# A diagonal state-space layer and an LSTM block: the order of work behind the last products

## The reference, cut to what matters

```python
x = L0_attn_r                                   # (8, 2048, 512) float32
x = x + _layernorm(_L0_attn_ref(_layernorm(x)))  # state-space convolution over the sequence, gelu
x = x + _layernorm(_L0_ffn_ref(_layernorm(x)))   # the block below
...
def step(c, xt):                                 # the scan runs over axis 0, of length 8
    ft = sigmoid(xt @ wf.T + c @ uf.T + bf)
    it = sigmoid(xt @ wi.T + c @ ui.T + bi)
    gt = tanh(xt @ wc.T + c @ uc.T + bc)
    return ft * c + it * gt, None
c_final, _ = lax.scan(step, c0, x)
h = tanh(einsum('tbi,oi->tbo', x, wo) + c_final @ uo.T + bo)
```

## Time and profile before

| | us |
|---|---|
| median of 3 executions | 2649.8 |
| lowest and highest of them | 2649.52 and 2650.55 |
| the profiled execution's own time | 2650.23 |
| its span, from the first to the last instruction | 2648.6 |
| TensorE busy (share of span) | 2526.6 (95%) |
| VectorE | 1841.0 (70%) |
| ScalarE | 1623.0 (61%) |
| GpSimd | 1133.2 (43%) |
| granted TensorE clock, mean, as a part of the full one | 0.982 |

### The profile page before, as it was taken

How to read it: one execution, slowest core, us unless ns; L and a number is a source line. 1 busy time by engine, 2 the same in 40 slices (tenths; PEclk the granted TensorE clock), 3 DMA queues, 4 the chain that set the end, 5 groups by cost and what they waited for, 6 DMA issues and landing times.

```text
span 2648.6 us, 57574 instructions
## 1 busy us (share of the span) xinstructions
PE 2526.6 (95%) x22659; PEld 2205.2 (83%) x22659; DVE 1841.0 (70%) x3413; ACT 1623.0 (61%) x3003; POOL 1133.2 (43%) x1437
## 2 busy tenths in 40 slices
PE   5499999997899999999999999999999999999997
PEld 4278888886788888888888888888888888888886
DVE  7855556558887677766777887776677764467666
ACT  8656667567665555555556665555555553378777
POOL 7768686725332223222234332322223220068667
PEclk9799999998999999999999999999999999999999
DMA  8779797889674556445655755544555432489998
GB/s 355 286 227 312 267 314 270 271 293 343 181 196 116 130 139 167 119 116 131 141 167 150 204 152 143 166 116 116 135 137 168 119 82 49 168 333 362 370 359 321
DMA packets 507551, 542.52 MB, mean 205 GB/s; under 512 B 273936, under 2 KB 412944, under 8 KB 488720
## 3 DMA queue, kind: packets, MB, share of 16 engines
q1 hardware_dynamic: 507280, 538.85, 65.3%
HBM read 292.88 MB, written 180.88 MB: 179 GB/s over the span
## 4 chain that ended last, share of the span: by engine, by line
PE 84%; DVE 4%; POOL 4%; ACT 3%; DMA 3%; issue 2%; SPq 1%; DVEq 0%; POOLq 0%; ACTq 0%
PE bank L2138 31%; PE bank L2148 29%; PE bank L2194 8%; PE bank L2027 4%; PE bank L1977 3%; PE bank L2013 3%; PE bank L2035 2%; PE bank L1989 2%; PE bank L2169 2%; DVE big L1827 1%; PE bank L1997 1%; ACT big L1343 1%; POOL big L886 1%; POOL big L990 1%; DVE big L1884 1%
## 5 line engine op out<-in xcount | busy, mean ns | idle before, releaser
L2138 PE MATMUL bank<-big 128*128 128x256 f16 x8064 | 1078.8, 273 | 20.8 <-ACT big L1387 8.3
L2148 PE MATMUL bank<-big 128*128 128x256 f16 x7056 | 962.5, 273 | 0.0
L2138 PEld LDWEIGHTS bank<-big 128*128 128x128 f16 x8064 | 790.4, 98 | 117.4 <-ACT big L1387 9.9
L2148 PEld LDWEIGHTS bank<-big 128*128 128x128 f16 x7056 | 690.4, 98 | 79.9
L1031 POOL TENSOR_SCALAR big<-big 128x1 f32<-128x1 f32 x253 | 108.0, 427 | 1084.8 <-DVE big L1674 806.4
L1884 DVE TENSOR_TENSOR big<-bank,big 128x512 f32<-128x512 f32 x256 | 175.1, 684 | 197.1 <-PE bank L2148 195.0
L2194 PE MATMUL bank<-big 128*128 128x256 f16 x2688 | 295.3, 273 | 4.4 <-ACT bank L1323 4.0
L1299 ACT ACTIVATE big<-big 128x512 f32<-128x512 f32 x384 | 289.6, 803 | 13.5 <-DVE big L1884 13.4
L2194 PEld LDWEIGHTS bank<-big 128*128 128x128 f16 x2688 | 262.4, 98 | 37.0 <-ACT bank L1323 4.9
L1870 DVE TENSOR_TENSOR big<-bank,big 128x512 f32<-128x512 f32 x256 | 176.3, 689 | 140.9 <-PE bank L2148 118.5
L1231 ACT ACTIVATE big<-big 128x512 f32<-128x512 f32 x256 | 205.9, 808 | 100.3 <-POOL big L1033 96.5
(11 more groups left out here) (233 smaller groups left out, 3724.3 us busy)
## 6 DMA issues: line engine op xcount, KB each, us to landing
xtd<-big SPq DMA_DIRECT2D x60, 1024.0 KB, 7.0
big<-xr SPq DMA_DIRECT2D x16, 2048.0 KB, 8.7
big<-xg SPq DMA_DIRECT2D x64, 512.0 KB, 7.8
big<-kpad SPq DMA_DIRECT2D x32, 1024.0 KB, 12.2
yd<-big SPq DMA_DIRECT2D x16, 2048.0 KB, 16.8
big<-x SPq DMA_DIRECT2D x128, 256.0 KB, 3.1
x1d<-big SPq DMA_DIRECT2D x128, 256.0 KB, 3.1
big<-x1d SPq DMA_DIRECT2D x64, 512.0 KB, 8.5
```

Of the source, the lines that this page charges most:

```text
L2138: ins = e.matmul(o, WX[2 * g + lw][:, q, kt, 128 * a:128 * a + 128], slot[u % 2][:, part, lx, k0 + kt, :], start=(first and kt == 0 and (l ...
L2148: ins = e.matmul(o, WC[2 * g + lw][:, q, kt, 128 * a:128 * a + 128], cc[unit(u)[1] % 2][:, qc, lx, kt, :], start=False, stop=end, skip_gro ...
```

## The change

Three edits behind the last products, and what they need in other places:

1. On VectorE, in turn m = 64, both closing sums of pair 63 come ahead of both statistics of pair 62.
2. On ScalarE, in turn m = 64, the tanh of pair 63 (both halves) comes ahead of the normalization of pair 61.
3. The residual sums of pairs 61 and 62 go from GpSimd to VectorE, behind all statistics and ahead of the sums of pair 63. SP waits for `hfin` for them. GpSimd makes the rates of pair 63 in one pass for both halves.

```diff
+POOL_PAIRS = PAIRS - 3
...
                 if m < PAIRS - 1:
-                    w.wait_ge(s["hres"], m + 1)
+                    if m < POOL_PAIRS:
+                        w.wait_ge(s["hres"], m + 1)
+                    else:
+                        w.wait_ge(s["hfin"], m - POOL_PAIRS + 1)
                     e.dma_start(o, rb[m % NRB]).then_inc(s[f"rb{m % NRB}"], 16)
                 else:
                     for r in range(2):
-                        w.wait_ge(s["hfin"], r + 1)
+                        w.wait_ge(s["hfin"], PAIRS - 1 - POOL_PAIRS + r + 1)
...
                 st = hst[:, m % 4]
-                parts = [slice(0, 2)] if m < PAIRS - 1 else [slice(0, 1), slice(1, 2)]
-                for part in parts:
-                    var = st[:, part, 7]
-                    w.wait_ge(s["hag"], 2 * m + part.stop)
...
+                var = st[:, :, 7]
+                w.wait_ge(s["hag"], 2 * m + 2)
...
             for m in range(PAIRS):
                 head_rates(m)
-                if m:
+                if 1 <= m <= POOL_PAIRS:
                     head_sum(m - 1)
...
-                if 0 <= m - 2 < PAIRS:
+                if 0 <= m - 2 < PAIRS - 1:
                     head_tanh(m - 2)
+                if m == PAIRS:
+                    head_tanh(PAIRS - 1)
...
-                if 0 <= m - 2 < PAIRS:
+                if 0 <= m - 2 < PAIRS and m != PAIRS:
                     head_stat(m - 2, 0)
...
-                if 0 <= m - 2 < PAIRS:
+                if 0 <= m - 2 < PAIRS and m != PAIRS:
                     head_stat(m - 2, 1)
...
+                if m == PAIRS:
+                    head_stat(m - 2, 0)
+                    head_stat(m - 2, 1)
...
+            for m in range(POOL_PAIRS, PAIRS - 1):
+                o = rb[m % NRB].rearrange("p r o -> p (r o)")
+                w.wait_ge(s["hn"], 2 * m + 2)
+                w.wait_ge(s[f"rb{m % NRB}"], 32 * (m // NRB) + 16)
+                e.tensor_tensor(o, zh[m % NZ].rearrange("p q t -> p (q t)"), o, ADD).then_inc(s["hfin"], 1)
             m = PAIRS - 1
```

More of the change, by code:

```diff
@@ L1068, in head_rates @@
                 st = hst[:, m % 4]
-                parts = [slice(0, 2)] if m < PAIRS - 1 else [slice(0, 1), slice(1, 2)]
-                for part in parts:
-                    var = st[:, part, 7]
-                    w.wait_ge(s["hag"], 2 * m + part.stop)
[L1073 to L1076, removed]
+                var = st[:, :, 7]
+                w.wait_ge(s["hag"], 2 * m + 2)
+                rp().tensor_scalar(var, var, EPS, None, ADD).then_inc(s["rp"], 1)
+                rp().tensor_tensor(var, var, mhalf.to_broadcast([128, 2]), ALU.pow).then_inc(s["rp"], 1)
+                for r in range(2):
+                    rp("rhm").tensor_scalar(st[:, r, 6:7], st[:, r, 6:7], st[:, r, 7:8], -1.0, MUL, MUL).then_inc(s["rhm"], 1)
             def head_sum(m):
```

## The result

| | before | changed |
|---|---|---|
| median of 20 executions | 2650.05 us | 2645.82 us |
| lowest and highest | 2649.0 and 2651.29 | 2644.94 and 2647.39 |
| ratio, 95% interval | | 0.9984, 0.9977 to 0.9991 |
| the profiled execution's own time | 2650.23 | 2646.91 |
| its span | 2648.6 | 2645.3 |

A forecast was written before the change was run, and what follows sets the result against it. TensorE's products were taken to bound the kernel until 2631.71 us. Last sum -2.63 and store tail -1.49 gave -4.1 from 2650.23, so 2646.1; that execution lay 0.4 above the median, hence 2645.7, range 2644.0 to 2647.8.

The forecast's parts named there:

- What the change can reach: Behind TensorE's last product at 2631.71 us: the change can act on about 16.9 us of the 2648.6 us span.
- Closing sums first: VectorE, pair 63: closing sums follow the sixth-product sum and last product, ending about 2632.4; last statistics end at 2635.74.
- the statistics' step: VectorE, pairs 62 and 63: each statistics instruction with its aggregation takes about 0.83 us, some 0.1 of it to the next.
- Tanh first: ScalarE: pair 63's tanh runs at 2631.8 and 2632.5, pair 61's normalization ends at 2634.65; no price while VectorE does statistics.
- Sums on VectorE: GpSimd loses two residual sums of 2.34 us and three small instructions; VectorE gains two of 1.22 us each.
- the second of the two ways: GpSimd's second scale for pair 62 precedes VectorE's sum of pair 61; pair 63's rates are then held, T = 2641.6.
- T: The end of VectorE's last residual sum: 2644.23 in the profile before, forecast 2641.6, 2.63 us earlier.
- The lockout: VectorE's sums with two SBUF operands hold GpSimd's small instructions for pair 63's rates; worst case 1.2 us more than taken.
- The tail: Stores behind the last sum: with the last half alone, the span ends 2.88 us after it instead of 4.37, worth 1.49.
- No lockout: Rival, chance 0.12: VectorE and GpSimd slip past each other, the last sum ends at 2639.7; -5.3 us, 2644.5.
- Smaller gain through late handovers: Rival, chance 0.20: last product usable later, or engine handovers 0.1 us longer each; gain -2 to -3.5, 2646.3 to 2647.8.
- Stretched sum: Rival, chance 0.03: VectorE's half sums take 1.97 us beside any GpSimd work; +1.8 us, 2651.6, slower than before.

The follow-up runs named there:

- e11: Changed kernel with normalized halves of pairs 61 to 63 in PSUM, stored by halves, and pairs 62 and 63's statistics ahead of their aggregations: 0.9978 of the time before.
- e3: Changed kernel with the tanh edit undone, the first and third edits kept: ratio to the kernel before 0.9985.
- e4: Changed kernel with VectorE's residual sums of pairs 61 and 62 cut to 8 of 1024 columns: ratio to the kernel before 0.9979.
- e7: Changed kernel with normalized halves of pairs 61 to 63 written to PSUM, so VectorE's sums read one SBUF operand; whole stores for pairs 61 and 62: ratio 0.9983.
- e5: Kernel before with GpSimd's last residual sum (pair 62) cut to 8 of 1024 columns: ratio to the kernel before 0.9994.
- e1: Only the first two edits, residual sums of pairs 61 and 62 left on GpSimd and pair 63's rates in halves: ratio to the kernel before 1.0.

## Why the prediction was right, point by point

The forecast was 2645.7 with -4.1 us; measured were 2645.82 and -4.23. Behind the last product, where the forecast's terms stand, 3.96 us were gained and 4.12 forecast, and the median of before moved from 2649.8 to 2650.05 with more executions; so the mechanism was right, but that the medians agree to 0.1 is in part luck.

- *What the change can reach.* Right: all of the difference between the profiles stands behind the last product. The profiled execution's span fell by 3.3 only, since its last product came 0.66 later.
- *Closing sums first.* Right for the sums: 0.73 behind the last product, forecast 0.7. **Mis-sized was the statistics' step**, "about 0.83" a half: the four took 0.93 to 1.04 from one to the next, the last ending at 4.55 and not at 4.03. The trace of before had it: pair 63's two statistics, between which nothing else stands, begin a whole microsecond apart, at 2634.62 and 2635.62:

```profile
2634.62 0.68 DVE L1827 BATCH_NORM_STATS2 big<-big 128x6 f32<-128x512 f32 x1
2635.34 0.18 DVE L1828 BATCH_NORM_AGGREGATE big<-big 128x2 f32<-128x6 f32 x1
```

The forecast's "some 0.1 to the next" holds only where the next instruction does other work. e11 shows the surplus to go when the instructions need not wait for their predecessors; in the older order another instruction filled that time.

- *Tanh first.* Right: no price, and by e3 no gain either.
- *Sums on VectorE.* Right: 2.34 us for both, unstretched, the long ones one behind the other. The tie that I left open did not arise, as the statistics came later; GpSimd's second scale was through at 2636.70, before VectorE's sum at 2636.84. What followed is the second of the two ways, step for step: the power ends 0.57 behind the second sum. The half microsecond that the statistics came late did not reach T whole: the second sum no longer had to wait for its normalization (that ended at 2637.90, and the first sum only at 2636.84 + 1.22 = 2638.06). Nothing in the forecast had provided for that; it was luck. T - last product is 10.02, forecast 2641.6 - 2631.71 = 9.89.
- *The lockout.* Right in kind (e4, e7) and size: I let it cost what moves T from 2639.7 to 2641.6, 1.9; e4 gives 1.70. As for the rule that the pair of ports is held for the whole instruction (the Trainium skill, "SBUF — State Buffer", Who interferes with whom): the rows show GpSimd as the one that waits, and VectorE as the one held where GpSimd's instruction is long (the 1.97 of before, gone in e5, and the 1.99 of e1). Whether a small one would hold VectorE stays open: in the changed kernel the power was begun at 2638.21, with VectorE's second sum already running, so the case didn't come up.
- *The tail.* Right: 2.91 behind T, forecast 2.88, and the sum of its terms, with the bytes counted from the store that bunches, holds for the twelve other profiles to 0.12. The estimate from the Trainium skill ("DMA: Bandwidth & Descriptors", Anatomy of one DMA), T + 3.45, whose fit is for DMAs that GpSimd issues, is half a microsecond too long for these stores of SP.
- *The rivals.* No lockout: out, by the rows of L1075 and L1076. Smaller gain through late handovers: the half microsecond was there, in the statistics, and was mostly hidden. Stretched sum: out by the two sums of 1024 in 2.34, and by e5's first half.

## What to carry to other kernels

Behind the last product of a kernel, list each engine's row and ask which one the last result stands in; moving work earlier on another engine brought nothing until that row was shortened, and 0.3 us behind it. A sum moved from GpSimd to VectorE held GpSimd's next instructions here when it read two SBUF operands; with one operand in PSUM it held none of them. Count the bytes from the last large store on as well: making the last result earlier brings nothing if the store before it moves closer, and storing by halves helps.

## What the runs showed of the hardware that I had not expected

- ScalarE's normalization to PSUM takes 1.48 us for two halves, hardly less than to SBUF (1.52), though its copies of 128x512 from SBUF to a bank take 0.59 each in the same loop.
- The end of the last product scatters from 2630.32 to 2633.22 over the profiles of thirteen runs in which the program up to there is the same in work. So the spans of two single executions can't show a difference of less than 3 us; the time behind the last product repeated to 0.05 in the two kernels profiled twice (12.93 and 12.92; 11.50 and 11.55).
